# Block 0 of a fused two-layer transformer kernel: attention scores on four row groups in one go, a new order of work, and the context split straight from PSUM

## What is computed

```python
qkv = h @ Wqkv + bqkv
q, k, v = jnp.split(qkv, 3, axis=-1)
x = x + _attn(q, k, v) @ Wos + bos
h = _ln(x, ln2_w, ln2_b) * (1 + sc2[:, None, :]) + sh2[:, None, :]
x = x + _attn(h @ Wq + bq, context @ Wk + bk, context @ Wv + bv) @ Woc + boc
```

## Time and profile before

| | us |
|---|---|
| median of 3 runs | 4212.19 (4211.66 to 4212.67) |
| the profiled execution | 4212.79 |
| its span, first to last instruction | 4210.6 |
| TensorE matmul busy | 4066.8 (97%) |
| VectorE busy | 2858.3 (68%) |
| ScalarE busy | 2751.7 (65%) |
| GpSimd busy | 2903.7 (69%) |

### The profile page before, as it was taken

One profiled execution on the slowest core, in us unless ns is written; L12 is line 12 of the kernel. 1 busy time (PEld: TensorE's weight loads), 2 busy tenths in 40 slices (PEclk: granted clock), 3 DMA queues, 4 the chain that ended last, 5 costly groups with the idle time before them and its releaser, 6 DMA issues.

```text
span 4210.6 us, 95756 instructions
## 1 busy us (share of the span) xinstructions
PE 4066.8 (97%) x34870; PEld 3478.2 (83%) x34870; DVE 2858.3 (68%) x6066; ACT 2751.7 (65%) x10788; POOL 2903.7 (69%) x2706
## 2 busy tenths in 40 slices
PE   7999999999999999999999999999999999999999
PEld 6777777777779988888888888888888888888998
DVE  7888888888865556565656565777776767664443
ACT  6999999999953336666666666666666666665333
POOL 5777788888767775666665665666666666666776
PEclk9999999999999999999999999999999999999999
DMA  2101111111111122212121212322222222221110
GB/s 83 32 32 32 32 45 39 43 47 47 50 54 46 61 63 78 82 70 81 71 81 70 80 71 96 105 78 90 85 83 87 83 86 81 89 98 55 41 51 31
DMA packets 230900, 276.64 MB, mean 66 GB/s; under 512 B 38044, under 2 KB 160416, under 8 KB 230432
## 3 DMA queue, kind: packets, MB, share of 16 engines
q1 hardware_dynamic: 230364, 270.51, 19.1%
q10 hardware_dynamic: 68, 0.02, 0.0%
HBM read 85.89 MB, written 50.33 MB: 32 GB/s over the span
## 4 chain that ended last, share of the span: by engine, by line
PE 76%; POOL 9%; DVE 7%; ACT 4%; issue 3%; DMA 0%; ACTq 0%; SPq 0%; DVEq 0%; POOLq 0%
PE BANKS L607 18%; PE BANKS L609 16%; PE BANKS L608 16%; PE BANKS L801 7%; PE BANKS L765 6%; PE BANKS L753 6%; POOL PR L1234 3%; PE BANKS L687 2%; ACT PR L904 2%; POOL Z L1277 2%; PE BANKS L823 2%; POOL HL L1244 1%; DVE WL L1095 1%; POOL X L1291 1%; DVE PT L1058 1%
## 5 line engine op out<-in xcount | busy, mean ns | idle before, releaser
L1234 POOL TENSOR_TENSOR PR<-PR,RL 128x512 f32<-128x512 f32 x1024 | 1067.8, 1047 | 657.7 <-DVE RL L1063 655.8
L920 ACT ACTIVATE PR<-BANKS,NM 128x128 f32<-128x128 f32 x2048 | 730.6, 382 | 443.6 <-DVE NM L1109 439.2
L904 ACT ACTIVATE PR<-BANKS,NM 128x128 f32<-128x128 f32 x2048 | 730.8, 412 | 12.5 <-DVE NM L1050 10.4
L607 PE MATMUL BANKS<-HH,WH 128*128 128x512 f32 x1632 | 689.0, 422 | 5.3 <-POOL HL L1239 2.7
L801 PE MATMUL BANKS<-ID,PR 128*128 128x128 f32 x4096 | 623.7, 275 | 59.3 <-POOL PR L1234 23.5
L1109 DVE TENSOR_REDUCE NM<-BANKS 128x8 f32<-128x1024 f32 x256 | 313.4, 1224 | 488.0 <-PE BANKS L765 488.0
L608 PE MATMUL BANKS<-HL,WH 128*128 128x512 f32 x1632 | 642.6, 394 | 0.0
L609 PE MATMUL BANKS<-HH,WL 128*128 128x512 f32 x1632 | 641.6, 393 | 0.0
L801 PEld LDWEIGHTS BANKS<-ID,PR 128*128 128x128 f32 x4096 | 487.3, 140 | 184.3 <-POOL PR L1234 66.5
L904 ACT ACTIVATION_READ_ACCUMULATOR PR<-BANKS,NM 128x1 f32 x2048 | 516.8, 253 | 0.0
L920 ACT ACTIVATION_READ_ACCUMULATOR PR<-BANKS,NM 128x1 f32 x2048 | 452.6, 221 | 0.0
(11 more groups left out here) (132 smaller groups left out, 10742.0 us busy)
## 6 DMA issues: line engine op xcount, KB each, us to landing
SW<-SN SPq DMA_DIRECT2D x1024, 128.0 KB, 2.1
x_scratch<-X SPq DMA_DIRECT2D x80, 512.0 KB, 3.1
X<-x_scratch SPq DMA_DIRECT2D x80, 512.0 KB, 4.0
CX<-in_ctx SPq DMA_DIRECT2D x32, 384.0 KB, 4.1
X<-in_x SPq DMA_DIRECT2D x16, 512.0 KB, 3.8
out<-X SPq DMA_DIRECT2D x16, 512.0 KB, 2.9
CX<-in_ctx SPq DMA_DIRECT2D x32, 128.0 KB, 4.3
STG<-in_L_xcond_W SPq DMA_DIRECT2D x4, 512.0 KB, 4.9
```

The source lines that it names most:

```text
L607: e.matmul(o, lh, rh, start=first and i == 0, stop=False)
L904: made = e.activation(pr[:, r], bank[:, r], ACT.Exp, bias=nm[:, h:h + 1], accum_out=RL[npr(t)[0]][:, h:h + 1])
L920: made = e.activation(pr[:, r], bank[:, r], ACT.Exp, bias=nm[:, h:h + 1], accum_out=RL[npr(t)[0]][:, h:h + 1])
L1234: e.tensor_tensor(p3, p3, RL[npr(t)[0]][:, :].unsqueeze(2).broadcast_to([128, 4, 128]), ALU.mult).then_inc(s_nrm, 1)
```

## The change

The schedule:

1. scores0 becomes one go for the whole batch at tb: 24 matmuls in the order c, k, r with r over all four row groups. It waits for all four exponential tiles of the batch before. The max for h = 0 and 1 is at tb and tb+1.
2. q and k are one tick earlier (tg-18 and tg-10), their high halves with them; the low halves are two ticks after the matmuls. On TensorE q and k stand at the end of a tick, behind p_turn, in place of ahead of v. The rotation of banks follows that order.
3. On ScalarE exp0 of tiles u = 1 to 3 is the first stage of its tick, and of u = 0 the last but the weight split. Before, all stood behind high0.
4. For p = 1 c_hf goes. VectorE makes HH (L1010's reduction) and HL (a subtraction) straight from PSUM, a tick earlier than c_split was, with semaphores of their own (s_hhc, s_hlc), and c_turn's bank comes free after HL. POOL's HL for the context goes.

What follows is bookkeeping: counters hfs and huse in place of counts over both kinds of parts.

```diff
@@ schedule
                     at["c_turn", tg - 16 + c if p == 1 else tg - 7].append(Part(p, g, c, 0))
-                    at["c_hf", tg - 15 + c if p == 1 else tg - 7].append(Part(p, g, c, 0))
-                    at["c_split", tg - 14 + c if p == 1 else tg - 6].append(Part(p, g, c, 0))
+                    if p == 4:
+                        at["c_hf", tg - 7].append(Part(p, g, c, 0))
+                    at["c_split", tg - 15 + c if p == 1 else tg - 6].append(Part(p, g, c, 0))
...
-                    tq, tk = (tg - 17 + 4 * j, tg - 9 + 4 * j) if (p, g) != (0, 0) else (tg - 17 + j, tg - 15 + j)
-                    tq += 2 * ((p, g) == (0, 1))
+                    tq, tk, late = (tg - 18 + 4 * j, tg - 10 + 4 * j, 2) if (p, g) != (0, 0) else (tg - 17 + j, tg - 15 + j, 1)
+                    tq += 4 * ((p, g) == (0, 1))
                     at["q", tq].append((p, g, j))
                     at["q_high", tq + 1].append((p, g, j))
-                    at["q_low", tq + 1].append((p, g, j))
+                    at["q_low", tq + late].append((p, g, j))
                     at["k", tk].append((p, g, j))
                     at["k_high", tk + 1].append((p, g, j))
-                    at["k_low", tk + 1].append((p, g, j))
+                    at["k_low", tk + late].append((p, g, j))
...
                 tb = tg + 4 * b
+                at["scores0", tb].append(Batch(p, g, b))
                 for h in range(2):
-                    at["scores0", tb + 2 * h - 2].append(Half(2 * (4 * (NG * p + g) + b) + h, p, g, b, h))
-                    at["max0", tb + 2 * h - 1].append(Half(2 * (4 * (NG * p + g) + b) + h, p, g, b, h))
+                    at["max0", tb + h].append(Half(2 * (4 * (NG * p + g) + b) + h, p, g, b, h))
@@ banks: the lines for q and k move from ahead of v to behind p_turn, and
+                    if stage == "c_turn" and x.p == 1:
+                        tp.add((stage, x), FOUR, s_hlc, 2 * x.g + x.c + 1)
+                        continue
@@ TensorE: the stages q and k move from behind scores0 to behind p_turn, and in scores0
-                    q.wait_ge(s_exp, 4 * (4 * ga + x.b) + 2 * x.h - 2)
+                    q.wait_ge(s_exp, 4 * (4 * ga + x.b))
                     for c in range(2):
                         for k, (qt, kt) in enumerate(((AH, KBH), (AH, KBL), (AL, KBH))):
-                            for r in (2 * x.h, 2 * x.h + 1):
+                            for r in range(4):
...
-                    made.then_inc(s_s0, 1)
+                    made.then_inc(s_s0, 2)
@@ ScalarE: exp0's body becomes a function
             for tick in ticks:
+                exponentials([t for t in at["exp0", tick] if t.u])
+
                 for p, g, j in at["q_high", tick]:
...
+                exponentials([t for t in at["exp0", tick] if not t.u])
+
                 for w, key, c in at["w_split", tick]:
@@ VectorE
                 for x in at["c_split", tick]:
                     u, k = h_of(x.p, x.g, True)
-                    q.wait_ge(s_hf, hparts["c_turn", x] + 1)
+                    if x.p == 1:
+                        bank = PS[tp.bank(("c_turn", x))]
+                        q.wait_ge(s_turn, hparts["c_turn", x] + 1)
+                        q.wait_ge(*hid.free((True, x.p, x.g)))
+                        rounded(HH[k][:, x.c, :], bank[:, :], x.p).then_inc(s_hhc, 1)
+                        q.wait_ge(s_hhc, 2 * x.g + x.c + 1)
+                        e.tensor_tensor(HL[k][:, x.c, :], bank[:, :], HH[k][:, x.c, :].bitcast(F), ALU.subtract).then_inc(s_hlc, 1)
+                        continue
+                    q.wait_ge(s_hf, hfs["c_turn", x] + 1)
```

More of the change, by code:

```diff
@@ L343, in build @@
         s_cst, s_cmv, s_cve, s_crs, s_cz = (sem(k) for k in ("cst", "cmv", "cve", "crs", "cz"))
-        s_turn, s_hf, s_hh, s_hl, s_hm = (sem(k) for k in ("turn", "hf", "hh", "hl", "hm"))
+        s_turn, s_hf, s_hh, s_hl, s_hm, s_hlc, s_hhc = (sem(k) for k in ("turn", "hf", "hh", "hl", "hm", "hlc", "hhc"))
         s_bias, s_res = sem("bias"), sem("res")
@@ L425, in build @@
                 if x.c == 0:
+                    if x.p == 4:
+                        huse[True, x.p, x.g] = len(huse)
                     hid.add((True, x.p, x.g), *((s_v, 4 * xq(x.p, x.g) + 4) if x.p == 1 else (s_v1, v_use(x.p, x.g, 8))))
@@ L429, in build @@
                 tp.add("modulation", (7,), s_mod, 3)
[L430 to L433, removed]
             for x in at["v", tick]:
@@ L452, in build @@
                 tp.add(("p", t.n), FOUR if t.n < NL0 else THREE, *pt_done(t))
+            for p, g, j in at["q", tick]:
+                tp.add(("q", p, g, j), FOUR, s_al, 2 * xq(p, g) + j + 1)
+            for p, g, j in at["k", tick]:
+                tp.add(("k", p, g, j), FOUR, s_kbl, 2 * xq(p, g) + j + 1)
             for stage in ("turn", "c_turn"):
@@ L455, in build @@
                     hparts[stage, x] = len(hparts)
-                    tp.add((stage, x), FOUR if x.p < 2 else THREE if KIND[x.p] == "b" else LATE if (x.p, x.g) == (2, 1) else TWO, s_hf, len(hparts))
+                    if stage == "c_turn" and x.p == 1:
+                        tp.add((stage, x), FOUR, s_hlc, 2 * x.g + x.c + 1)
+                        continue
+                    hfs[stage, x] = len(hfs)
+                    tp.add((stage, x), FOUR if x.p < 2 else THREE if KIND[x.p] == "b" else LATE if (x.p, x.g) == (2, 1) else TWO, s_hf, len(hfs))
             for x in at["out", tick]:
@@ L468, in h_of @@
         def h_of(p, g, context=False):
-            return hid.at[context, p, g], hid.slot((context, p, g))
+            return huse.get((context, p, g), g), hid.slot((context, p, g))
         def wview(buf, key):
@@ L802, in _ @@
                     made.then_inc(s_t, 1)
+                for p, g, j in at["q", tick]:
+                    u, h = h_of(p, g)
+                    key = "Wq" if p == 1 else "Wqkv"
+                    q.wait_ge(s_hl, 2 * u + 2)
+                    q.wait_ge(s_wlo, w_ready[key])
+                    q.wait_ge(*tp.free(("q", p, g, j)))
+                    project_t(key, 128 * j, h, PS[tp.bank(("q", p, g, j))]).then_inc(s_q, 1)
+                for p, g, j in at["k", tick]:
+                    u, h = h_of(p, g, p == 1)
+                    key, col0 = ("Wk", 0) if p == 1 else ("Wqkv", 256)
+                    q.wait_ge(s_hlc if p == 1 else s_hl, 2 * u + 2)
+                    q.wait_ge(s_wlo, w_ready[key])
+                    q.wait_ge(s_bk, 2)
+                    if p == 1:
+                        q.wait_ge(s_hm, cq(p, g) + 1)
+                    q.wait_ge(*tp.free(("k", p, g, j)))
+                    bank = PS[tp.bank(("k", p, g, j))]
+                    e.matmul(bank[:, :], BK[:, p, 128 * j:128 * j + 128], ONES[:, :], start=True, stop=False)
+                    project_t(key, col0 + 128 * j, h, bank, False).then_inc(s_k, 1)
                 for x in at["out", tick]:
@@ L871, in _, with exponentials @@
                     e.dma_start(CROWB[r + 1:r + 2, 64 * i:64 * i + 64], a[key][128:CD].unsqueeze(0)).then_inc(s_crows, 16)
+            def exponentials(tiles):
+                for t in tiles:
+                    q.wait_ge(s_nm0, t.n // 2 + 1)
+                    q.wait_ge(s_t, t.n - NP0 + 1)
+                    q.wait_ge(s_nrm, t.n - NP0 + 1)
+                    bank, pr, nm = PS[t.u], PR[npr(t)[0]], NM0[t.n // 2 % 3][:, 4 * (t.n % 2):4 * (t.n % 2) + 4]
+                    for h in range(4):
+                        r = slice(128 * h, 128 * h + 128)
+                        made = e.activation(pr[:, r], bank[:, r], ACT.Exp, bias=nm[:, h:h + 1], accum_out=RL[npr(t)[0]][:, h:h + 1])
+                    made.then_inc(s_exp, 1)
             for tick in ticks:
+                exponentials([t for t in at["exp0", tick] if t.u])
                 for p, g, j in at["q_high", tick]:
@@ L895, in _ @@
                     e.activation(OH[vi % 3][:, :, :], PS[tp.bank(("pv", x))][:, 0:256].rearrange("p (c t) -> p c t", c=2), ACT.Copy).then_inc(s_oh, 1)
[L897 to L903, removed]
-                        made = e.activation(pr[:, r], bank[:, r], ACT.Exp, bias=nm[:, h:h + 1], accum_out=RL[npr(t)[0]][:, h:h + 1])
-                    made.then_inc(s_exp, 1)
                 for x in at["low", tick]:
@@ L1160, in _ @@
                     u, k = h_of(x.p, x.g)
-                    q.wait_ge(s_hf, hparts["turn", Part(x.p, x.g, x.c, 1 if KIND[x.p] == "a" else 0)] + 1)
+                    q.wait_ge(s_hf, hfs["turn", Part(x.p, x.g, x.c, 1 if KIND[x.p] == "a" else 0)] + 1)
                     q.wait_ge(*hid.free((False, x.p, x.g)))
```

12 lines of the change are left out of this document (5 added, 7 removed).

## The result

The changed kernel takes 4560.6 us (median, 4554.6 to 4569.2) against 4211.9 (4210.5 to 4212.7): 1.083 times the time of before, 95% interval 1.0816 to 1.0842, or 349 us slower. The profiled execution took 4556.4 us, its span 4554.4. The forecast was 4475 with a range of 4330 to 4570.

The account below looks back on a forecast made before the run. Two nearly full in-order queues, TensorE and ScalarE, were taken to bound block 0, held together by overlapped halves. Self attention +127 and cross attention +136 gave +263 us on 4212: 4475 us, range 4330 to 4570.

Parts of the forecast that it names:

- Scores: TensorE's 24 score matmuls in one go: four row groups at 0.117 us per four, 0.90 us saved per batch.
- rival C: Score matmuls on four row groups take 0.234 us per four: +0.7 per batch, +90 us, 4565 us; chance 0.08.
- The new wait: Scores wait for all four exponentials; next exponential 2.25 us after scores start (T), ScalarE idle about 1.2 us per q batch.
- The loops of the batches: Self attention's group of four batches: 42.8 us against 34.88, +7.9 per group, +127 us.
- b0: First batch of a self-attention group: out0 6.27 us after scores start, q waits to about 7.9; 9.9 us.
- b1: Second batch of a self-attention group: k in place of q, one more matmul, 0.24 us more; 9.2 us.
- b2: Third batch of a self-attention group: turn waits for a ScalarE copy behind k_high, to 12.4 us; next scores 12.7.
- b3: Fourth batch of a self-attention group: PV waits for k_low (4.25 us), q for POOL's HL to 9.0; 11.0 us.
- the sum: Total over block 0: self attention +127, cross attention +136, together +263 us, giving 4475 us; chance 0.60.
- A: Only the base loop counts, slips in order hide most additions: 4245 us, with half of them 4360; chance 0.22.
- B: ScalarE paces block 0 at 34.9 to 35.0 us per group: 4196 us, half the gain about 4204; chance 0.10.
- The cross attention: First batch's out0 waits for VectorE's HH and HL, to 8.1 us; group 44.6 against 36.1, +8.5, +136 us.

Follow-up runs that it names:

- experiment 9: The changed kernel with 12 unread matmuls of 512 columns on TensorE, once per group, in the wait before the fourth batch's PV: 4523.7 us.
- experiment 10: The changed kernel with the 12 filler matmuls before PV of experiment 9, and four each in the waits of v and out0: 4547.9 us.
- experiment 11: The changed kernel with k_low a tick earlier, one tick after k as before the change: 4540.4 us.
- experiments 3 and 6: On the kernel before: 3, only the direct rounding and splitting of the context, 4207.3 us; 6, scores in one go and that direct split, 4507.9 us.

## Why the prediction was right in sign and short in size

**Scores.** Right, and rival C is dead: 404.39 to 404.61 is the first step, then 404.73, so four matmuls on four row groups every 0.12 us after the first step, as fast as two before. From the first score matmul to PV are 0.91 us (417.11 to 418.02). But the 0.90 us saved per batch bought a chain scores, max, exponentials in which each waits for the one before.

The forecast cites two rules from the Trainium skill, TensorEngine Tiling (Array Packing). Theoretical Speedup: the runs agree as far as they go, since four row groups do twice the work of two in the same time; one row group alone was not run. PSUM Bottleneck: they agree, since the 24 matmuls take 0.91 us, the max behind them 1.22, and the first exponential starts 2.29 us after the first score matmul.

**The new wait.** Foreseen at T+2.25 for the first exponential. ScalarE and VectorE of the changed kernel, T = 404.39:

```profile
405.42 1.22 DVE L1061 TENSOR_REDUCE NM<-BANKS 128x8 f32<-128x1024 f32 x1 [4.63 <-PE BANKS L696]
...
406.68 0.37 ACT L890 ACTIVATE PR<-BANKS,NM 128x128 f32<-128x128 f32 x1 [1.31 <-DVE NM L1061]
```

T+2.29, and ScalarE idle for 1.31 (foreseen 1.2).

**The loops of the batches.** This is the group from 404.39. b0 was to have out0 at 6.27 and q at 7.9 and to take 9.9: it had 6.28, 7.88 and 9.90. b1: out0 5.97, 9.36 us (foreseen 9.2). b2: transpose u=2 at T+6.50, turn at T+12.54 on ScalarE's PT copy, 12.91 us (foreseen 12.4 and 12.7); ScalarE's rows show the order that was to cause it:

```profile
447.10 0.69 ACT L909 ACTIVATE WH<-BANKS,MASK 128x512 fp32r<-128x512 f32 x1 [1.09 <-PE BANKS L618]
447.69 0.68 ACT L910 ACTIVATE WH<-BANKS,MASK 128x512 fp32r<-128x512 f32 x1
448.26 0.60 ACT L952 ACTIVATE PT<-BANKS 128x512 f32<-128x512 f32 x1
```

The copy (L952) stands behind the two halves of the masked k, although its transpose (444.83, 0.63 us long) was done 2.8 us before. b3: PV at T+4.28 (foreseen 4.25), then 12.72 us against 11.0. In p=1 out0 of b0 waits as foreseen for the HL that now stands on VectorE, at T+8.15 (foreseen 8.1), and the batch takes 11.68 (foreseen 11.6).

**Where the sum was short.** It priced every instruction behind a new wait with a duration from the earlier trace rows, that is at the clock of a TensorE that is never idle for long. There was no term for the clock, though the text itself foresaw PV at 4.25 us in b3, and so over 3 us of standing. With the batches at full clock, as the change or experiment 9 shows them, the groups are 9.90 + 9.36 + 12.91 + 11.20 = 43.4 and 11.68 + 9.75 + 12.71 + 11.20 = 45.3 us.

The sum also started from a wrong group of p=1. It read 36.1 us from all max reductions between 664 us and the end of the block, and the last batches there are shorter than the rest; a group in the middle takes 36.6. With it the sum would have been about 255 us and not 263, so this slip hid a little of the shortfall. Then, by the mean groups:

- at full clock 16 x (43.4 - 34.9) + 16 x (45.3 - 36.6) = about 275 us. The 20 above 255 are seven slips of 0.1 to 0.3 us, one in each batch but the b0 of p=0.
- the half clock, 16 x (45.6 - 43.4) + 16 x (47.8 - 45.3) = about 75 us. This is the missing term. The batches which are longer in some groups than in others are those with a granted clock below 1.00: b0 of p=0 takes 9.90 us at 1.00 and 11.0 at 0.85, b2 12.9 at 1.00 and 13.9 at 0.88.
- that makes 350 us; the odd groups at the ends bring it to the 343.8 of the two traces.

The split of the waits from the clock rests on experiment 9 for b3 and for b1 of p=1, on the changed kernel's own groups for the rest. How much a kernel would gain whose clock never dropped and which did nothing else differently is not shown: experiment 10 held the clock up in p=0 but paid for it on the path. The nearest is experiment 11, where the same instructions of a p=0 group take 42.96 us at 1.00 and 45.8 with the drop.

**The rivals.** A (most of the additions hidden, 4245 or 4360) is wrong: the four batches of a group differ as foreseen. B (ScalarE paces) is wrong too: it idles about 1.3 us in each batch before its first exponential (47.8 us in 38 waits). C gave the nearest number, 4565, by a mechanism that isn't there. A number near the result is no support for its reason.

**The cross attention.** Its direct split was put at no cost for what it takes off ScalarE and POOL and at the wait of out0 on HL; experiments 3 and 6 show that this price depends on the scores: 5 us gained beside two goes, 46 lost beside one, the half clock in p=1 included.

## What to carry to other kernels

A wider go of matmuls that needs all the banks of its readers turned overlapped work into a chain here, and work put on the queue that starts each turn of that chain (VectorE) then cost time that it had not cost before. Sum the chain of one batch from its first instruction, and if TensorE comes out idle for microseconds in it, price what follows at half its clock too. Read such times from the mean over many groups: in the changed kernel one group of p=0 is up to 2.4 us off another, and twice a single group misled here. And try each part of a change beside the others: the same edit was worth 5 us gained or 46 lost, and the same order 0 or 238.

## What the runs showed of the hardware

- Four row groups of 32x256 matmuls go at 0.12 us per four, the pitch that two such matmuls on two row groups had.
- TensorE's granted clock fell to 0.51 for about 5.5 us after it had stood 3.30 us once per group (PV 1.94 us in place of 1.08). With the other drops it cost about 75 us of block 0's time.
- With that one idle stretch filled or removed, drops stayed or came up in other batches of the group, where each single wait is shorter (at most 2.2 us).
- In the changed kernel itself the drop also occurs behind two waits of about 1 us: in p=1's b1 in nearly every group, and in p=0's b2 in each third group. The first row is of such a b2, which starts at 390.45, the second of a b1 of p=1:

```profile
396.96 1.07 PE L789 MATMUL BANKS<-ID,PR 128*128 128x128 f32 x4 [1.00 <-DVE OL L1113]
...
944.11 1.05 PE L789 MATMUL BANKS<-ID,PR 128*128 128x128 f32 x4
```

The b2 one group later runs the same instructions behind the same waits (1.24 and 1.00 us in the group of 396.96, 1.23 and 1.01 in this one, the row of 442.87 above) and keeps 1.00: its four transposes take 0.63 us and not 1.07.

Neither the longest single wait nor the waits of the batch itself are thus enough to tell where the clock falls; what exactly decides it, these runs don't settle.
